# Attention kernel: one reduction over two PSUM banks, scores in three single banks, sums in two halves of columns

## What is computed

```python
def _L1_attn_ref(x, Wq, bq, Wk, bk, Wv, bv):
    q = jnp.einsum('bsd,de->bse', x, Wq) + bq
    k = jnp.einsum('bsd,de->bse', x, Wk) + bk
    v = jnp.einsum('bsd,de->bse', x, Wv) + bv
    scores = jnp.einsum('bqd,bkd->bqk', q, k) / jnp.sqrt(jnp.asarray(d, x.dtype))
    attn = jax.nn.softmax(scores, axis=-1)
    out = jnp.einsum('bqk,bkd->bqd', attn, v)
    return out + x

x = x + _L0_conv_ref(_gn(x), ...)
t = _to_tokens(x)
t = t + _L1_attn_ref(_ln_t(t), ...)
t = t + _L1_ffn_ref(_ln_t(t), ...)
```

## Time and profile before

| | us |
|---|---|
| median of 3 runs | 2791.23 |
| lowest and highest | 2777.22, 2791.93 |
| profiled execution, first to last instruction (span) | 2788.9 |
| of it PE busy, DVE busy, ACT busy | 2406.2, 2339.7, 1600.3 |
| attention, first scores to last copy | 582.9 to 2270.8 |

### The profile page before, as it was taken

The page is one execution under the profiler, slowest core; times in us unless marked ns, Lnnn a source line. Parts: engine busy times, 40 slices in busy tenths (PEclk is TensorE's granted clock), DMA queues, the critical chain, the costliest instruction groups (busy, mean ns, idle before and its releaser), DMA issues. The chain is left out here.

```text
span 2788.9 us, 46984 instructions
## 1 busy us (share of the span) xinstructions
PE 2406.2 (86%) x18454; PEld 959.6 (34%) x18454; DVE 2339.7 (84%) x4150; ACT 1600.3 (57%) x2106; POOL 396.3 (14%) x456
## 2 busy tenths in 40 slices
PE   3888878379999999999999999999999987766775
PEld 1343333122222222222222222222222246655663
DVE  4567776699999999999999999999999927777777
ACT  1143343247777777777777777777777753233323
POOL 0021121300000000000000000000000004444445
PEclk9989989579999999999999999999999986666766
DMA  7687692500210230211211201201200011222221
GB/s 173 171 221 221 192 270 97 177 24 1 59 50 10 59 107 17 59 38 22 59 33 28 59 24 36 59 18 42 59 7 19 24 62 55 70 75 100 70 70 24
DMA packets 68110, 206.29 MB, mean 74 GB/s; under 512 B 20630, under 2 KB 33554, under 8 KB 61234
## 3 DMA queue, kind: packets, MB, share of 16 engines
q1 hardware_dynamic: 64034, 185.27, 24.1%
q0 software_dynamic: 3040, 15.57, 1.5%
q10 hardware_dynamic: 816, 2.46, 0.3%
HBM read 80.14 MB, written 61.31 MB: 51 GB/s over the span
## 5 line engine op out<-in xcount | busy, mean ns | idle before, releaser
L1331 DVE TENSOR_REDUCE at_XM<-at_psX 128x1 f32<-128x448 f32 x2688 | 1546.2, 620 | 90.1 <-PE at_psX L1182 69.3
L1248 ACT ACTIVATE at_PR<-at_psS 128x896 f32<-128x896 f32 x1344 | 1163.1, 915 | 452.3 <-PE at_psS L1158 450.3
L1200 PE MATMUL at_psV<-at_PR,at_V 128*32 128x448 f32 x5376 | 644.8, 551 | 0.1
L1158 PE MATMUL at_psS<-at_US,at_KS 128*128 128x448 f16 x2688 | 636.1, 356 | 0.6 <-ACT at_PR L1248 0.2
L1182 PE MATMUL at_psX<-at_KS,at_US 64*128 64x448 f16 x1344 | 490.2, 365 | 64.8 <-DVE at_XM L1331 42.9
L1182 PE MATMUL at_psX<-at_KS,at_UH 64*128 64x448 f16 x1344 | 490.3, 365 | 0.0
L1182 PEld LDWEIGHTS at_psX<-at_KS,at_US 64*128 64x128 f16 x1344 | 124.6, 93 | 720.5 <-DVE at_XM L1331 661.4
L1158 PEld LDWEIGHTS at_psS<-at_US,at_KS 128*128 128x128 f16 x2688 | 200.9, 98 | 273.1 <-ACT at_PR L1248 119.4
L1297 POOL CAST at_mrow<-at_mt 7x128 f16<-7x128 f32 x64 | 18.0, 281 | 1611.0 <-DVE at_mt L1350 1258.2
L1588 POOL TENSOR_TENSOR fi_WE<-fi_WE 128x256 f32<-128x256 f32 (+1 forms) x224 | 202.5, 935 | 179.7 <-DVE fi_WE L1641 179.6
L1641 DVE TENSOR_TENSOR fi_WE<-fi_psE,fi_WT 128x512 f32<-128x512 f32 (+1 forms) x208 | 134.2, 666 | 74.4 <-PE fi_psE L1495 73.3
(11 more groups left out here) (200 smaller groups left out, 2050.4 us busy)
## 6 DMA issues: line engine op xcount, KB each, us to landing
sums<-at_O SPq DMA_DIRECT2D x16, 1568.0 KB, 6.3
fi_SUMS<-sums SPq DMA_DIRECT2D x16, 1568.0 KB, 6.5
sb_stacks<-sb_T SPq DMA_DIRECT2D x64, 270.5 KB, 7.6
sb_stacks<-sb_Xp SPq DMA_DIRECT2D x64, 248.8 KB, 9.7
sb_stacks<-sb_Xp SPq DMA_DIRECT2D x64, 248.0 KB, 5.8
sb_stacks<-sb_T SPq DMA_DIRECT2D x64, 172.5 KB, 10.8
at_KS<-key_stacks SPq DMA_DIRECT2D x32, 208.0 KB, 6.8
fi_RES<-residual SPq DMA_DIRECT2D x16, 400.0 KB, 7.0
```

The lines of the kernel that those rows point to most:

```text
L1158: last = nc.tensor.matmul(psS[:, at % 2, k, 0:TILE], KS[:, b, (2 * c + k) * P:(2 * c + k + 1) * P], US[:, b, t * TILE:(t + 1) * TILE], sta ...
L1200: last = nc.tensor.matmul(psV[C * q:C * q + C, 0:TILE], V[:, b, G * k + q, :], PR[:, (n * 2 * STEPS + 2 * q4 + q // 2) % PRS, q % 2, :], s ...
L1248: nc.scalar.activation(PR[:, f % PRS], psS[:, at % 2, :, 0:TILE], ACT.Exp).then_inc(p_ready, 1)
L1331: nc.vector.tensor_reduce(o, psX[:, (at + j) % 3, 0:TILE], AX.X, ALU.max).then_inc(x_done, 1)
```

## The change

PSUM is dealt out anew: `psS` has three single banks (`SBANKS`), `psX` two slots of two banks. On DVE one `tensor_reduce` of 128 x (2 x 448) takes the two maxima of a pair into two neighbouring columns of `XM`, which is laid out by unit. A pair counts once in `x_full` and `x_done`. A score chunk is a slot of its own: one matmul, one exponential of 448 columns, one count in `s_full` and `p_ready`. `sums` is called twice for each quad, for columns 0 to 223 and 224 to 447. The second call of a tile's last quad adds the half chunk. `keep` follows the fourth exponential of its step. The new order on PE is scores 0, pair, scores 1, sums (first half), half scores, scores 2, pair, scores 3, sums (second half), third pair.

```diff
-        SLOTS = 2 * STEPS + PARTS
+        QUAD = 4 * STEPS
-        PRS = 8
+        PRS = 16
+        SBANKS = 3
-        PR = sb("PR", [P, PRS, 2, TILE])
+        PR = sb("PR", [P, PRS, TILE])
-        XM = sb("XM", [P, NT, NF])
-        XE = sb("XE", [P, PARTS])
+        XM = sb("XM", [P, UNITS])
-        psS = ps("psS", [P, 2, 2, 512])
-        psX = ps("psX", [P, 3, 512])
+        psS = ps("psS", [P, SBANKS, 512])
+        psX = ps("psX", [P, 2, 2, 512])
...
+            def scores(n, s, k):
+                b, at, (t, c) = n % B, score_place(n, s, k), divmod(4 * s + k, NF)
+                if k == 0 and s % PSTEPS == 0:
                     pe.wait_ge(m_in, rows_in(n, s // PSTEPS))
-                if at >= 2:
-                    pe.wait_ge(p_ready, at - 1)
-                for k in range(2):
-                    last = nc.tensor.matmul(psS[:, at % 2, k, 0:TILE], KS[:, b, (2 * c + k) * P:(2 * c + k + 1) * P],
-                                            US[:, b, t * TILE:(t + 1) * TILE], start=True, stop=True)
-                last.then_inc(s_full, 1)
+                if at >= SBANKS:
+                    pe.wait_ge(p_ready, at - SBANKS + 1)
+                nc.tensor.matmul(psS[:, at % SBANKS, 0:TILE], KS[:, b, c * P:(c + 1) * P],
+                                 US[:, b, t * TILE:(t + 1) * TILE], start=True, stop=True).then_inc(s_full, 1)
...
             def maxima(m, i):
-                if at + 1 >= 3:
+                if at >= 2:
                     pe.wait_ge(x_done, at - 1)
...
-                    o = psX[:, (at + j) % 3, 0:TILE]
+                    o = psX[:, at % 2, j, 0:TILE]
...
-                    last.then_inc(x_full, 1)
+                last.then_inc(x_full, 1)
...
-            def sums(n, q4):
+            def sums(n, q4, half):
                 b, (t, k) = n % B, divmod(q4, QUADS)
-                pe.wait_ge(p_ready, slot(n, q4, 1) + 1)
-                if k == 0 and n * NT + t >= 1:
-                    pe.wait_ge(o_ready, n * NT + t)
+                a, z = half * TILE // 2, (half + 1) * TILE // 2
+                if half == 0:
+                    pe.wait_ge(p_ready, score_place(n, q4, 3) + 1)
+                    if k == 0 and n * NT + t >= 1:
+                        pe.wait_ge(o_ready, n * NT + t)
                 for q in range(G):
+                    last = nc.tensor.matmul(psV[C * q:C * q + C, a:z], V[:, b, G * k + q, :], PR[:, ring_of(n, q4, q), a:z],
+                                            start=(k == 0 and half == 0), stop=(k == QUADS - 1), skip_group_check=True)
+                if half == 1:
+                    last.then_inc(p_used, 1)
...
+                    q = n * STEPS + s - LAG
                     scores(n, s, 0)
                     if len(pairs) >= 1:
                         maxima(*pairs[0])
-                    q = n * STEPS + s - LAG
+                    scores(n, s, 1)
                     if q >= 0:
-                        sums(*divmod(q, STEPS))
+                        sums(*divmod(q, STEPS), 0)
                     if s % PSTEPS == 0:
                         half_scores(n, s // PSTEPS)
+                    scores(n, s, 2)
                     if len(pairs) >= 2:
                         maxima(*pairs[1])
-                    scores(n, s, 1)
+                    scores(n, s, 3)
+                    if q >= 0:
+                        sums(*divmod(q, STEPS), 1)
                     if len(pairs) >= 3:
                         maxima(*pairs[2])
...
-                nc.scalar.activation(PR[:, f % PRS], psS[:, at % 2, :, 0:TILE], ACT.Exp).then_inc(p_ready, 1)
+                nc.scalar.activation(PR[:, f % PRS], psS[:, at % SBANKS, 0:TILE], ACT.Exp).then_inc(p_ready, 1)
...
                 for s in range(STEPS):
-                    exponentials(n, s, 0)
+                    for k in range(4):
+                        if k == 2 and s % PSTEPS == 0:
+                            half_exponentials(n, s // PSTEPS)
+                        exponentials(n, s, k)
                     m, q4 = divmod(n * STEPS + s - LAG, STEPS)
                     if m >= 0 and q4 % QUADS == QUADS - 1:
                         keep(m, q4 // QUADS)
-                    if s % PSTEPS == 0:
-                        half_exponentials(n, s // PSTEPS)
-                    exponentials(n, s, 1)
...
-                for j in range(2):
-                    c, t = unit(2 * i + j)
-                    dve.wait_ge(x_full, at + j + 1)
-                    o = XE[:, t:t + 1] if c == NF else XM[:, t, c:c + 1]
-                    nc.vector.tensor_reduce(o, psX[:, (at + j) % 3, 0:TILE], AX.X, ALU.max).then_inc(x_done, 1)
+                dve.wait_ge(x_full, at + 1)
+                nc.vector.tensor_reduce(XM[:, 2 * i:2 * i + 2], psX[:, at % 2, :, 0:TILE], AX.X, ALU.max).then_inc(x_done, 1)
```

More of the change, by code:

```diff
@@ L1017, in place @@
         def place(m, i):
-            return (m * (UNITS + PARTS) + 2 * i + sum(last_pair(p) + DELAY < i for p in range(PARTS - 1))
+            return (m * (XPAIRS + PARTS) + i + sum(last_pair(p) + DELAY < i for p in range(PARTS - 1))
                     - (m >= 1 and i < DELAY))
@@ L1022, in turn_place @@
             if p < PARTS - 1:
-                return place(m, last_pair(p) + DELAY) + 2
-            return place(m + 1, DELAY - 1) + 2 if m + 1 < N else place(m, XPAIRS - 1) + 2
+                return place(m, last_pair(p) + DELAY) + 1
+            return place(m + 1, DELAY - 1) + 1 if m + 1 < N else place(m, XPAIRS - 1) + 1
         def ends_at(m, i):
@@ L1047, in first_pairs, with score_place, half_place, ring_of @@
             return [divmod(g, XPAIRS) for g in range(LEAD)]
[L1050 to L1054, removed]
+        def score_place(n, s, k):
+            return n * (QUAD + PARTS) + 4 * s + s // PSTEPS + k + (s % PSTEPS > 0 or k >= 2)
+        def half_place(n, p):
+            return n * (QUAD + PARTS) + p * (4 * PSTEPS + 1) + 2
+        def ring_of(n, s, k):
+            return (n * QUAD + 4 * s + k) % PRS
         def half_tiles(bank):
@@ L1189, in turn_max @@
                 at = turn_place(m, p)
-                pe.wait_ge(x_done, at - 2)
+                pe.wait_ge(x_done, at - 1)
                 pe.wait_ge(negm_ready, turned_parts(m, p))
-                nc.tensor.transpose(psX[0:chunks_of(p), at % 3, 0:P], negm[:, p, 0:chunks_of(p)], ident[:]).then_inc(x_full, 1)
-            def sums(n, q4):
+                nc.tensor.transpose(psX[0:chunks_of(p), at % 2, 0, 0:P], negm[:, p, 0:chunks_of(p)], ident[:]).then_inc(x_full, 1)
+            def sums(n, q4, half):
                 b, (t, k) = n % B, divmod(q4, QUADS)
-                pe.wait_ge(p_ready, slot(n, q4, 1) + 1)
-                if k == 0 and n * NT + t >= 1:
-                    pe.wait_ge(o_ready, n * NT + t)
-                for q in range(G):
[L1200 to L1204, removed]
+                a, z = half * TILE // 2, (half + 1) * TILE // 2
[3 more added lines that the diff above has]
+                        pe.wait_ge(o_ready, n * NT + t)
+                for q in range(G):
+                    last = nc.tensor.matmul(psV[C * q:C * q + C, a:z], V[:, b, G * k + q, :], PR[:, ring_of(n, q4, q), a:z],
+                                            start=(k == 0 and half == 0), stop=(k == QUADS - 1), skip_group_check=True)
+                if half == 1:
+                    last.then_inc(p_used, 1)
+                if k == QUADS - 1 and half == 1:
                     w = TILE // G
@@ L1231, in _ @@
             for q in range(N * STEPS - LAG, N * STEPS):
-                sums(*divmod(q, STEPS))
+                for half in range(2):
+                    sums(*divmod(q, STEPS), half)
         @block.scalar
@@ L1240, in half_exponentials, with exponentials @@
                     act.wait_ge(v_full, (n - 1) * NT + min(2 * p + 2, NT))
-                nc.scalar.activation(PL[:, p], psS[:, at % 2, 0, 0:TILE], ACT.Exp).then_inc(p_ready, 1)
-            def exponentials(n, s, i):
-                at, f = slot(n, s, i), n * 2 * STEPS + 2 * s + i
+                nc.scalar.activation(PL[:, p], psS[:, at % SBANKS, 0:TILE], ACT.Exp).then_inc(p_ready, 1)
+            def exponentials(n, s, k):
+                at, f = score_place(n, s, k), n * QUAD + 4 * s + k
                 act.wait_ge(s_full, at + 1)
                 if f >= PRS:
-                    act.wait_ge(p_used, (f - PRS) // 2 + 1)
-                nc.scalar.activation(PR[:, f % PRS], psS[:, at % 2, :, 0:TILE], ACT.Exp).then_inc(p_ready, 1)
+                    act.wait_ge(p_used, (f - PRS) // 4 + 1)
+                nc.scalar.activation(PR[:, f % PRS], psS[:, at % SBANKS, 0:TILE], ACT.Exp).then_inc(p_ready, 1)
             def keep(n, t):
```

25 lines of the change are left out of this document (12 added, 13 removed).

## The result

The changed kernel takes 3039.98 us (median of 4 runs) against 2791.58 before: the ratio is 1.093, 95% interval 1.088 to 1.098. It is 9% slower; 3055 was forecast, in a range of 3005 to 3105. The profiled execution has a span of 3034.2 us. Of the runs listed for the experiments, one of the kernel before (4344.78 us) and one of the last version (4334.10 us) fell in a slower state of the chip and are left out.

A forecast was written before the change was run, and what follows sets the result against it. PE was taken to bound the attention. 302 + 2 - 38 + 6 - 3 - 6 = +263 us on the 2788.9 us span gave 3052, or 3055 us as median time, 9% slower; range 3005 to 3105.

The forecast's parts named there:

- The bound: Attention: PE sets the step of 2.345 us, with DVE some 0.17 us a step behind it.
- equal distances with and without maxima: PE timeline: scores to sums 0.86 us, sums to scores 0.89, the same at the attention's end where DVE is idle.
- The step: PE in the attention: eight runs in place of four, 2.80 us against 2.345, +0.46 a step, +302 us over 656 steps.
- The lower and upper bounds of half a V: Half the sums on PE, taken as 0.515 us: 0.50 at least; above, some 0.04 more if second weight loads show.
- 302 + 2 - 38 + 6 - 3: Attention, us: full steps +302, last 16 steps +2, DVE stalls gone -38, transposes +6, third pairs -3.
- The transposes: 64 in the attention: each loses a 0.17 us wait, but the pair after waits some 0.1 for its bank: +6 us.
- The pairs ahead: 32 pairs of maxima before the attention, 1.27 us each, fall to about 1.08 with two pairs of banks: -6 us.
- the long reduction: DVE: one reduction of 896 elements takes 1.11 us, where two of 448 took 1.16.
- the copy's margin of 0.2 us: Copy of the sums done 1.0 us after the first L1207 matmul; PE has 1.19 us of other work until then.
- the second rival: New waits at 112 copies (0.2 us) and 96 transposes and third pairs (0.5 us) add 70 us: 3125 us; chance 7%.
- The first: Rival: PE's form changes cost nothing, DVE bounds at 2.11 to 2.21 us a step: about 2660 us; chance 4%, 1% even.
- The third rival: PE's granted clock drops to 1.2 GHz from 2.4, each step gaining 1.88 us: +1230 us, 4290 us; chance 2%.

The follow-up runs named there:

- the last version: Changed kernel with scores in twos, both pairs together, sums whole, transposes and third pairs moved to the step's end, sums mid-step in the last 16 steps: 2759.84 us.
- the versions with four runs a step: Changed kernel's banks, reduction and exponentials, order two scores, two pairs, two scores, whole sums: 2824.16 us; with transposes, third pairs and late sums moved: 2759.84 us.

## Why the prediction was right

**The bound.** PE, not DVE: shown from three sides. DVE's busy time went down by 80 us and the attention went up by 262; splitting the reduction again moved nothing in the changed kernel; and the versions with four runs a step have the shorter DVE work too, yet their step is 2.34 to 2.35 us, the 2.345 of before and no less. The reading that led there, equal distances with and without maxima, holds.

**The step.** 2.80 us forecast, 2.80 measured, each run to the hundredth (0.295, 0.295, 0.295, 0.515 against 0.29, 0.30, 0.29, 0.52). This is the term that carries the forecast, and it came out by its mechanism. The lower and upper bounds of half a V weren't needed: the second weight loads stay hidden.

**The terms.** The attention was to gain 302 + 2 - 38 + 6 - 3 = 269 us and gained 262.4; a step off by 0.01 us would be 6.6. The transposes are the term that was wrong in kind: the sum had an even 0.1 us of waiting at each, but three in four wait for nothing and one in four, behind a third pair, waits some 0.8 us. That they cost in all about what the sum had is partly luck: the 39 that wait for nothing are cheaper than forecast (0.29 us behind their pair, where 0.53 less 0.17 was taken), and the 13 are dearer. The pairs ahead took 8.3 us less, for 6 forecast: two follow one another by 1.00 us there, where 1.08 was taken.

```profile
570.62 0.55 PE L1184 MATMUL at_psX<-at_KS,at_US 64*128 64x448 f16 x1 [0.44 <-DVE at_XM L1337]
...
571.62 0.55 PE L1184 MATMUL at_psX<-at_KS,at_US 64*128 64x448 f16 x1 [0.44 <-DVE at_XM L1337]
```

Of the 17.8 us between the 3052 forecast for the span and the 3034.2 measured, 6.6 lie in the attention and 2.3 in the pairs ahead. The other 8.8 us lie in stages that the change doesn't touch (the start of the first pair 2.5 us earlier, what is behind the attention 6.3 us shorter).

**DVE, ACT and the copy.** 1.11 us forecast for the long reduction, 1.09 measured; 543 ns for the exponential of 448, as its neighbour of the same size had it; the copy's margin of 0.2 us held, 0.5 us lost in all. Where that margin was removed, V waited 0.38 us at a copy: the second rival's mechanism is real, but in this order it came to 0.5 us at copies and some 13 at transposes (10.8 us in 1580, estimated for the whole), not to 70.

**The rivals.** The first (a change of form costs nothing of its own) fell in every kernel with another number of runs a step and no wait in the step that is read: eight take 2.80 us, six 2.60 and 2.55, four 2.34, and with all X and S over full rows the loss between these two is gone. The Trainium skill says in TensorE: Matmul & The Clock Gate, Part 3, What overlaps and what doesn't, that a weight load overlaps matmuls in flight only when it goes to other rows of the array. Here it does so for the same rows too, where the matmuls divide the array alike (S to S, and X to S over all rows: loads 0.19 us ahead of their matmuls), and it does not where the division changes (the load at 1302.21 with its matmul at 1302.22); the measurement decides. So the loads are not hidden at a border. Whether the 0.1 us is the load itself (93 to 108 ns in the groups) or an emptying of the array, for which the load stands back, was not separated. The third rival did not come: the granted clock stayed at 1.0 from 572.1 to 2522.4 us.

**What the change lost, then:** its own gain, 0.07 us a pair on DVE, lies off the path; its price comes of the order on PE that was chosen for three single banks. These banks rule out four scores together without a wait, not four runs a step: with the scores in twos, the two pairs one behind the other and the sums whole, the same banks give all of it back and a little more.

## What to carry to other kernels

Before a busy second engine is believed to be the bound, look for a stretch where it has nothing to do and see whether the first engine's distances change. Count on TensorE not matmuls but runs of matmuls that divide the array alike: each border was worth about 0.11 us here (0.46 us for four), and the same work with eight borders a step instead of four took 9% more of the whole. When an instruction is moved, look at what frees its bank: four of the experiments lost time to a copy, a pair or a transpose that had stayed where it was.

## What the runs showed that was not expected

Sums of 224 columns in two halves, with every weight load doubled, cost nothing (ratio 1.001) as long as the halves stand together. At a change of form the next weights are not loaded ahead, though the profile shows nothing that the load waits for. Sums of float32 over the full 128 columns take 0.95 us to a following pair of 64-row matmuls but 0.75 us to a following full-size float16 matmul. And in the ring of three banks two pairs stood 1.08 us apart at the closest, with the second waiting for DVE; where PE's order puts less than that between them, spacing the pairs evenly is worth time.
